# Two edge passes of a graph network: matmul signals moved onto drains

## What is computed

```python
logits = leaky_relu(a_src[src] + a_dst[dst])      # attn: einsum(q[dst], k[src]) * scale
m = segment_max(logits, dst); e = exp(logits - m[dst])
alpha = e / segment_sum(e, dst)                   # typed: alpha *= edge_weight
out = segment_sum(h[src] * alpha, dst)
```

## Time and profile before

| what | value |
|---|---|
| time, median of 3 runs (lowest to highest) | 4023.26 us (4017.4 to 4023.55) |
| span of the profiled execution, its only time shown | 4831.1 us |
| mean granted TensorE clock in it | 0.788 |
| PE / PE loads / DVE / ACT / POOL busy, share of the span | 63% / 45% / 64% / 30% / 56% |
| DMA | 561.56 MB, mean 116 GB/s |

### The profile page before, as it was taken

The page is one execution under the profiler, slowest core; times in us unless marked ns, Lnnn a source line. Parts: engine busy times, 40 slices in busy tenths (PEclk is TensorE's granted clock), DMA queues, the critical chain, the costliest instruction groups (busy, mean ns, idle before and its releaser), DMA issues. The chain is left out here.

```text
span 4831.1 us, 70737 instructions
## 1 busy us (share of the span) xinstructions
PE 3023.5 (63%) x14389; PEld 2152.2 (45%) x14389; DVE 3082.1 (64%) x9652; ACT 1461.7 (30%) x4590; POOL 2703.3 (56%) x2963
## 2 busy tenths in 40 slices
PE   5344455555557567777777778834555565656998
PEld 4233333333345344444445455523333343434998
DVE  6455666666667545555555556846666777778786
ACT  2222222222225434445545455500001011101333
POOL 3556665555550245666555552565666666653787
PEclk9667777777778877888888888967777777777999
DMA  4544444444432433333333343643444444443221
GB/s 135 150 120 132 132 134 130 131 134 130 127 112 89 131 94 107 111 110 109 104 102 110 104 113 96 209 134 106 121 122 125 117 123 124 120 121 86 68 71 53
DMA packets 290341, 561.56 MB, mean 116 GB/s; under 512 B 85318, under 2 KB 183278, under 8 KB 289998
## 3 DMA queue, kind: packets, MB, share of 16 engines
q0 software_dynamic: 115872, 326.30, 24.3%
q10 hardware_dynamic: 101462, 168.49, 11.4%
q1 hardware_dynamic: 72664, 63.00, 4.5%
HBM read 479.67 MB, written 77.89 MB: 115 GB/s over the span
## 5 line engine op out<-in xcount | busy, mean ns | idle before, releaser
L464 PE MATMUL psum<-big,onehots_or_distances 128*128 128x264 f32 (+2 forms) x5280 | 1889.5, 485 | 314.6 <-issue 143.2
L464 PEld LDWEIGHTS psum<-big,onehots_or_distances 128*128 128x128 f32 x5280 | 1065.1, 233 | 554.9 <-issue 266.0
L278 POOL DMA_INDIRECT big<-table_attn,src_by_edge x782 | 741.1, 948 | 751.2 <-SPq L271 343.3
L668 DVE TENSOR_TENSOR acc<-acc,psum 128x264 f32 (+2 forms) x1320 | 559.4, 424 | 872.7 <-remote 404.2
L278 POOL DMA_INDIRECT big<-table_gat,src_by_edge x782 | 770.3, 985 | 528.0 <-SPq L271 289.1
L278 POOL DMA_INDIRECT big<-table_typed,src_by_edge x782 | 772.9, 988 | 483.0 <-SPq L271 242.4
L427 PE MATMUL psum<-big,onehot_t 128*128 x2640 | 510.4, 308 | 245.1 <-issue 132.8
L447 PE MATMUL psum<-growth,ones 64*128 64x4 f32 (+2 forms) x330 | 89.5, 341 | 901.1 <-DVE growth L610 855.6
L510 DVE SCALAR_TENSOR_TENSOR dot_products<-psum,big 128x258 f32<-128x258 f32 x880 | 364.4, 421 | 421.2 <-PE psum L427 240.8
L645 DVE TENSOR_TENSOR big<-big,psum 128x512 f32<-128x512 f32 x880 | 594.3, 675 | 9.6 <-issue 0.5
L447 PEld LDWEIGHTS psum<-growth,ones 64*128 64x128 f32 (+2 forms) x330 | 74.8, 281 | 980.6 <-DVE growth L610 923.5
(11 more groups left out here) (284 smaller groups left out, 4101.0 us busy)
## 6 DMA issues: line engine op xcount, KB each, us to landing
onehot_t<-onehots ACTq DMA_DIRECT2D x73, 512.0 KB
big<-visit_positions ACTq DMA_DIRECT2D x55, 512.0 KB
onehots<-big ACTq DMA_DIRECT2D x37, 512.0 KB
big<-onehots ACTq DMA_DIRECT2D x37, 512.0 KB
big<-in_x_dram SPq DMA_DIRECT2D x98, 128.0 KB, 2.7
big<-table_gat,src_by_edge POOLq DMA_INDIRECT x782
big<-table_attn,src_by_edge POOLq DMA_INDIRECT x782
big<-table_typed,src_by_edge POOLq DMA_INDIRECT x782
```

Source lines behind the costliest of these rows:

```text
L278: pool.indirect_dma_start(X[:, t % RING, :], None, ph.table, bass.IndirectOffsetOnAxis(ap=m.src[:, t:t + 1], axis=0)).then_inc(S[f"rows{t ...
L464: last = nc.tensor.matmul(sum_ps(w), onehot_at(v), rows, start=(v % 2 == 0), stop=(v % 2 == 1))
L668: nc.vector.tensor_tensor(row, row, sum_ps(w), ALU.add).then_inc(S["added"], 1)
```

## The change

In the first and third pass the increment of `summed` no longer sits on the second matmul of a pair, and that of `expanded` no longer on the last spreading matmul of a batch: each is carried by a drain of TensorE that follows the matmul. The second pass keeps both on the matmuls (its spreadings return earlier in `expand`).

```diff
                 last = nc.tensor.matmul(expanded_at(g), spreading, ph.tab[:, bass.ds(blk, 1), :, :].rearrange("p a s k -> p (a s k)"), start=True, stop=True)
                 if g == G - 1:
-                    last.then_inc(S["expanded"], 1)
+                    pe.drain().then_inc(S["expanded"], 1)
...
                 last = nc.tensor.matmul(sum_ps(w), onehot_at(v), rows, start=(v % 2 == 0), stop=(v % 2 == 1))
-                if v % 2:
+                if v % 2 and ph.dot:
                     last.then_inc(S["summed"], 1)
+                elif v % 2:
+                    pe.drain().then_inc(S["summed"], 1)
```

## The result

| | before | after |
|---|---|---|
| median | 4020.33 us (4 runs, 4014.9 to 4023.55) | 4279.88 us (4 runs, 4257.81 to 4304.52) |
| ratio, 95% interval | 1 | 1.0649 (1.0621 to 1.0677) |
| span of the profiled execution | 4831.1 us | 4297.9 us |
| mean granted clock | 0.788 | 0.78 |

A forecast was written before the change was run, and what follows sets the result against it. Gathers were taken to bound the kernel at 1051 us a pass; with drains PE at 1.2 GHz needs 24.4 us a batch, 1382 us a pass, so 4023 + 662 = 4685, forecast 4690 us, range 4010 to 4900.

The forecast's parts named there:

- What bounds the kernel: All three edge passes: ordinary executions run at the gathers' pace, 1051 us a pass, 23 us above the floor.
- the 808 us of the shown span: Profiled span minus median: nearly all late-signal stalls were taken to belong to the profiled execution alone.
- step of 1.25 us: Edge passes: gathers come every 0.946 + 0.30 us, setting a 978 us floor and 17.8 us a batch.
- The signal of a matmul came late: DVE's adds in the edge passes: stalls are late matmul signals, about one a batch.
- The cost of a drain: PE, first and third pass: 0.46 us per drain at 1.2 GHz, 0.32 at 2.4, from lost overlap, drain, step, weight load.
- Each first in an even visit and so right behind a drain: PE's four register loads a batch, 0.54 us each, come into the open: 2.4 us with 0.06 us to use each register.
- PE at 1.2 GHz throughout: First and third pass: PE needs 24.4 us a batch against 17.8 us of gathers, adding 331 us a pass.
- I see nothing that lifts it: PE's clock, first and third pass: starts low and stays at 1.2 GHz, since drains prevent packing; adds 662 us.
- the clock still alternates: Rival for PE's clock in both drained passes: 4103 us at 44% high clock, 4385 at 20%; range 4050 to 4500, chance 0.22.
- main case: PE binds the first and third pass at the low clock: 4690 us, own range 4500 to 4900, chance 0.52.
- The page's estimate: PE's drains at the skill's 183 ns per isolated matmul: 21.9 us a batch at 1.2 GHz, about 4410 us.
- faster: Rival at DVE's adds: drain signals end late matmul signals in ordinary executions too; 3977 us, down to about 3800; chance 0.14.

The follow-up runs named there:

- second profile: The kernel before, unchanged, profiled once more: 4017.96 us in one run, span 4016.1 us.
- silent drains: The kernel after with increments back on the matmuls and the same drains kept behind them without a signal: 4307.12 us, ratio 1.0726.

## Why the prediction was wrong, point by point

- **What bounds the kernel: right.** The gathers, and the 808 us of the shown span as stalls of that execution, at 1051 us a pass. Measured 1056, 1020 and 1061. Their step of 1.25 us was too short, though: I took the median of 0.946 us, where 770 to 773 us of POOL in 782 gathers are 0.99 each. The second profile has them 1.3 us apart, so the room for PE was about 18.6 us a batch and not 17.8. "The signal of a matmul came late" isn't shown, as said above; the forecast doesn't use it.
- **The cost of a drain: right at 1.2 GHz, a little short at 2.4.** I had a plain pair grow by 0.32 us and a sequencer step of 0.05 at 2.4 GHz; it grew by 0.46. At 1.2 GHz a spreading pair should take 2.32 + 0.46 + 0.60 + 0.05 = 3.43 us; it takes 3.36. "Each first in an even visit and so right behind a drain" holds, and the loads weigh more than their 2.4 us a batch: with them out of the way the same nine drains cost 10 us of the 260.
- **PE at 1.2 GHz throughout: 24.4 us a batch forecast, 23.7 measured.** The first pass has stretches of this kind. Two starts of the same instruction one batch apart, and a window of four batches around them:

```profile
907.34 0.21 DVE L620 TENSOR_TENSOR shifted<-logit,psum 128x64 f32<-128x64 f32 x1
...
931.06 0.21 DVE L620 TENSOR_TENSOR shifted<-logit,psum 128x64 f32<-128x64 f32 x1
```

```profile
883.60:978.50 94.90, 78.59 (x209) 0.50 0.45 129
```

- **The failed step: "I see nothing that lifts it".** The sum took 1.2 GHz for both passes throughout. The clock does come back. Windows of PE through one batch of the third pass, columns as in the earlier trace rows:

```profile
3298.40:3305.20 6.80, 4.72 (x22) 0.99 0.45 112
3305.30:3311.90 6.60, 4.94 (x16) 0.50 0.59 190
3311.90:3318.80 6.90, 6.51 (x18) 0.51 0.42 112
3318.90:3325.70 6.80, 4.66 (x21) 0.99 0.49 114
```

In the spreading stretch, 3305.3 to 3311.9, PE is busy 4.94 of 6.60 us at 1.2 GHz and the clock stays. From 3311.9 on come the last spreading pair, plain pairs and the turns, busy 6.51 of 6.90 us, and then 2.4 GHz is granted. I had counted the plain pairs as nearly as open as the spreading ones: at 1.2 GHz a plain pair's hole is 0.23 us beside 2.15 us of matmuls, and the turns follow without a drain. But this doesn't say when the clock comes back: the four batches at 1.2 GHz above hold the same plain pairs and turns (PE is busy 6.56 us of the 6.90 from 904.2 on), and nothing lifted it there. What decides stays open. The rival "the clock still alternates" is what happened. Its own formula with the clock as granted, 0.63 and 0.67 (26 and 34% at 2.4 GHz), gives 1/(0.26/15.0 + 0.74/24.4) = 21.0 and 20.1 us a batch, passes of 1195 and 1146 us, and 4020 + 139 + 85 = 4244 us; measured 4280, with passes of 1233 and 1163 us. Long register loads would fill most of the 38 us that lack in the first pass: 28 of its 220 took over 1 us, 156 us in all where the kernel before had 122 (this line has all three passes).

```profile
L407 PEldq TENSOR_LOAD <-index x660: 528/545/2318, 147.0 to 3864.2; - x165
```

So what a drain costs stands, and the term that failed is the share of the high clock: zero forecast, 26 and 34% measured. That gave 662 us where 260 were measured. The measured time lies below the main case's own 4500 to 4900 and in the range of the rival, which had a chance of 0.22; the granted clock came out between the 0.5 to 0.6 that I named as a sign for my case and the 0.7 against it.
- **The page's estimate** (the Trainium skill, "TensorE: Matmul & The Clock Gate", Single matmul latency: 4410 us) used the same wrong clock. Its constant is small for a drain: 183 ns against the 0.46 us by which a plain pair grew. That it comes nearer to 4280 than my sum is luck: one error against the other. Its section HAM oscillation blames waits for DMAs; my reading, that short gaps by drains then wouldn't cost the high clock, is not borne out: with holes of 0.23 and 0.83 us the first pass went from 0.77 to 0.63. "PSUM — Partial Sum Buffer", Engine vs sequencer instructions, of the Trainium skill gives correctness as the reason to keep the increment on the matmul, and no price. The silent drains show that the price is the drain's and not that of where the increment sits: the increments were on the matmuls there, and the loss was the same.
- **The rival "faster"** fell with the second profile of before, which, as long as the unprofiled runs, has no such stalls for a drain to cure.

## What to carry to other kernels

A drain on TensorE cost more here than the wait for the last matmul: what the sequencer did in the shadow of queued matmuls (register loads, semaphore steps) came into the open behind it. Look for that first; moving four loads ahead took back 95% of the loss, and putting the signal back on the matmul takes back all of it. Where a profiled span stands far above the runs, profile again before costing its stalls; and where PE is near the pace of the kernel, work out both clocks and what share of each the busy stretches earn.

## What the runs showed of the hardware that I had not expected

- Extra matmuls made the slow kernel faster, 4280 to 4188 us, by raising the granted clock from 0.63 and 0.67 to 0.93 and 0.97; on the kernel before 880 extra matmuls were free.
- A drain with nothing to wait for costs TensorE 0.08 us, and one such a batch added some 60 us to the kernel with pair drains.
- With nine drains a batch, 48 of 54 batches of the third pass last 20.3 to 20.7 us, each with 6.8 us at 2.4 GHz; with eight, 8 or 17 do.
- Register loads of TensorE take 0.54 us, but in the first pass after, 28 of 220 took over 1 us and up to 2.3.
- One profiled execution took 4831 us against 4016 for the same program, and its trace has under half of the semaphore updates; what sets this off stays open.
